# A gated delta-rule recurrence on one core: the third block of the older row turned first, and ScalarE's line in another order

## What is computed

```python
q, k, v = (silu(conv4(x @ W.T) + b) for W, b in ...)     # k also times 64 ** -0.5
a = sigmoid(x @ Wa.T + ba)                               # a decay for every value column
beta = sigmoid(x @ Wb.T + bb)
def step(S, ins):
    q_t, k_t, v_t, a_t, b_t = ins
    read = einsum('bhk,bhkv->bhv', k_t, S)
    err = read - v_t
    S = a_t[:, :, None, :] * S - b_t[:, :, None, None] * k_t[..., None] * err[:, :, None, :]
    return S, einsum('bhk,bhkv->bhv', q_t, S)
o = layernorm(o) * ln_w + ln_b
o = (o * sigmoid(x @ Wg.T)) @ Wo.T
```

## Time and profile before

| what | us |
|---|---|
| median of three runs | 1928.45 |
| the profiled execution, device time | 1928.56 |
| its span in the trace | 1926.7 |
| busy PE, PEld | 1698.9, 1438.6 |
| busy DVE, ACT, POOL | 1402.2, 1002.4, 703.8 |

### The profile page before, as it was taken

How to read it: one execution, slowest core, us unless ns; L and a number is a source line. 1 busy time by engine, 2 the same in 40 slices (tenths; PEclk the granted TensorE clock), 3 DMA queues, 4 the chain that set the end, 5 groups by cost and what they waited for, 6 DMA issues and landing times. The chain is left out here.

```text
span 1926.7 us, 42128 instructions
## 1 busy us (share of the span) xinstructions
PE 1698.9 (88%) x15318; PEld 1438.6 (75%) x15318; DVE 1402.2 (73%) x3422; ACT 1002.4 (52%) x2618; POOL 703.8 (37%) x1037
## 2 busy tenths in 40 slices
PE   4599999899999999999988598999999999988795
PEld 3477778787887878777776465788888888768794
DVE  4688777877788777887774475677777777754577
ACT  2355655555555655555543354566666666641353
POOL 5455345543555335543451121122222222223553
PEclk9799999999999999999988798999999999998798
DMA  6122331223222332323311793111111111123222
GB/s 215 54 55 64 75 86 49 69 62 81 66 55 65 74 86 53 69 64 75 86 48 21 164 123 1 24 34 35 35 34 35 34 34 35 34 45 108 58 85 76
DMA packets 168772, 123.69 MB, mean 64 GB/s; under 512 B 44372, under 2 KB 148888, under 8 KB 167672
## 3 DMA queue, kind: packets, MB, share of 16 engines
q1 hardware_dynamic: 166072, 115.87, 28.1%
q0 software_dynamic: 2496, 5.13, 0.8%
HBM read 102.83 MB, written 18.12 MB: 63 GB/s over the span
## 5 line engine op out<-in xcount | busy, mean ns | idle before, releaser
L590 POOL TENSOR_TENSOR kfull<-kt,pair_rows 128x512 f32<-128x512 f32 x128 | 143.4, 1121 | 517.6 <-ACT kt L378 513.9
L358 PE MATMUL ps<-xT,taps 128*128 128x128 f32 x2048 | 277.7, 279 | 0.1
L850 ACT COPY wt<-ps 32x128 f32<-32x128 f32 x512 | 131.2, 256 | 263.9 <-PE ps L745 257.7
L1658 POOL TENSOR_TENSOR b_yT<-b_yT,b_recipT 64x256 f32<-64x256 f32 x128 | 110.0, 859 | 431.0 <-ACT b_yT L1609 422.4
L358 PEld LDWEIGHTS ps<-xT,taps 128*128 128x128 f32 x2048 | 259.4, 197 | 7.6 <-issue 7.2
L893 DVE TENSOR_TENSOR prod<-ps,mt 128x128 f32<-128x128 f32 x512 | 147.4, 288 | 78.4 <-PE ps L756 62.8
L1676 DVE TENSOR_REDUCE b_nmax<-ps 128x1 f32<-128x128 f32 (+7 forms) x256 | 194.1, 758 | 8.8
L745 PE MATMUL ps<-ident,w 128*128 128x128 f32 x512 | 162.9, 318 | 35.0 <-ACT wt L850 18.5
L896 DVE TENSOR_REDUCE w<-prod 128x32 f32<-128x128 f32 x512 | 146.6, 286 | 17.5
L1603 ACT ACTIVATE b_prob_long<-ps,b_nmax 128x1024 f32<-128x1024 f32 (+3 forms) x128 | 122.1, 954 | 70.7 <-DVE b_nmax L1676 70.7
L745 PEld LDWEIGHTS ps<-ident,w 128*128 128x128 f32 x512 | 87.9, 172 | 85.1 <-DVE w L896 74.5
(11 more groups left out here) (302 smaller groups left out, 3834.6 us busy)
## 6 DMA issues: line engine op xcount, KB each, us to landing
decay<-ends_dram SPq DMA_DIRECT2D x256, 128.0 KB
b_recipT<-recips_dram SPq DMA_DIRECT2D x64, 256.0 KB, 3.8
gn<-near_dram SPq DMA_DIRECT2D x32, 384.0 KB, 6.8
slots_dram<-zero SPq DMA_DIRECT2D x1, 9216.0 KB, 65.4
rr<-rates_dram SPq DMA_DIRECT2D x32, 256.0 KB, 4.5
sq<-rstd_dram SPq DMA_DIRECT2D x16, 512.0 KB, 3.7
wtap<-in_taps SPq DMA_DIRECT2D x4, 1024.0 KB, 11.7
f_w<-in_f_w SPq DMA_DIRECT2D x2, 2048.0 KB, 10.6
```

Source lines behind the costliest of these rows:

```text
L358: mm = pe.matmul(part, lhsT=taps[:, tap, t * P:(t + 1) * P], rhs=xT[:, :, columns(at_next) - LOOK + tap:columns(at_next) - LOOK + tap + TS ...
L590: nc.gpsimd.tensor_tensor(kfull[:, n % 4, :, :], kt[:, n % 2, :].unsqueeze(1).to_broadcast([P, G, P]), cst["pair_rows"][:, :].unsqueeze(2) ...
L850: nc.scalar.copy(wt[rows, b, :], ps[rows, 2, 0:P]).then_inc(wt_kept[b], 1)
```

## The change

Four things, all in the order of work; nothing is computed otherwise, and one tiny evaluation per block is added.

1. **PE's line.** The older row's turn 2 comes first, then `start` of the younger row, then take-off 2, and slot 0 only behind it.
2. **The ring.** Item `a1` goes from slot 3 of j = 1 to slot 0 of j = 2, in front of `wo`, and `a3` from slot 3 of j = 2 to slot 0 of j = 3, in front of `g0`.
3. **ACT's line.** `put_back` goes from the end of a half chunk to right behind `keep` 2. The diagonal factors go from j = 3 and 4 to j = 5 and 7.
4. **The table of Silu.** At the end of j = 4 ACT evaluates Silu on one column into a new tile, `ready`.

```diff
+        ready = sb("ready", [P, NS])
...
-                ["q0.0"], ["q0.1"], ["b", "a0"], ["n", "a1", "p1"],
-                ["wo.0"], ["wo.1"], ["a2"], ["a3", "p2"],
-                ["g0.0"], ["g0.1"], ["c0"], ["p3"],
+                ["q0.0"], ["q0.1"], ["b", "a0"], ["n", "p1"],
+                ["a1", "wo.0"], ["wo.1"], ["a2"], ["p2"],
+                ["a3", "g0.0"], ["g0.1"], ["c0"], ["p3"],
...
+                    if cy >= 0:
+                        turn(cy, y, 2)
                     start(cc, x)
                     if cy >= 0:
-                        turn(cy, y, 2)
+                        take_off(cy, y, 2)
                     ring(0)
-                    if cy >= 0:
-                        take_off(cy, y, 2)
                     turn(cc, x, 0)
...
                         keep(cy, y, 2)
+                    if cc >= 1:
+                        put_back(cc - 1, x)
                     ring(0)
...
-                    if cc >= 1:
-                        put_back(cc - 1, x)
                     if j == 0:
                         act_norm(act, both, f)
-                    if j in (3, 4) and f < NS - 1:
-                        act_diagonal(act, f, 1 - f % 2, j - 3)
+                    if j == 4 and f < NS - 1:
+                        nc.scalar.activation(ready[:, f:f + 1], cst["eps"][:, 0:1], ACT.Silu)
+                    if j in (5, 7) and f < NS - 1:
+                        act_diagonal(act, f, 1 - f % 2, (j - 5) // 2)
```

## The result

| | before | after |
|---|---|---|
| median, us (4 runs each) | 1928.42 | 1982.32 |
| lowest and highest | 1924.8 to 1928.5 | 1978.1 to 1983.98 |
| first to last group of state products in the trace | 964.72 | 1018.08 |
| one block of the recurrence (median) | 61.16 | 64.66 |

The account below looks back on a forecast made before the run. PE was taken to have the least slack, with 80.5 us of waits on DVE and ACT. A loss of 2.85 us per block, 42.8 us in fifteen blocks, plus 4 in the last, on 1928.6 gave about 1975 us; range 1934 to 2002.

Parts of the forecast that it names:

- likeliest case: Whole kernel: a loss, with a time between 1955 and 1990 us; chance 0.6, giving the forecast of 1975 us.
- What bounds the kernel: Recurrence: PE has the least slack, waiting 80.5 us; no order of the same work can win more than 80 us.
- PE's line: Heads: the turn ahead of start costs +0.83 or +0.84 us at j = 0, 4, 5; little at j = 1, 2, 6, 7.
- four late heads: Heads of j = 0, 3, 4, 5, where DVE's reduce ends after PE is free: 0.84, 0.4, 0.4, 0.1 us per block.
- The term of j = 1: At j = 1 only start covers ACT's norm; take-off 2's wait becomes 0.8 us, adding 0.25 us.
- `a1`: The product of j = 1 stops waiting (0.8 us), but the later drain delays DVE in j = 2: gain 0.1 us.
- `a3`: At j = 3 PE stalls 0.77 us and take-off 0 is held back some 0.35 us; j = 3 adds 0.4.
- Table load: At the end of j = 4 the load costs nothing; j = 5 gains 0.65 us and loses 0.83 at its head.
- Diagonal factors: At j = 6 take-off 2 waits about 0.35 us for them; +0.55 us taken there and +0.4 in j = 7.
- The clock case: Head of j = 0: a 2.1 us stall lowers the clock every block, 1.5 us more each, 1999 us; chance 0.08 with worse.
- The faster case: Heads: new stalls replace ones that come anyway, what is freed stays free, 2.1 us per block, 1896 us; chance 0.13.

Follow-up runs that it names:

- e7: The changed kernel with DVE's solve 2 of the next older row put in front of update: 1941.43 us, 1.016 of the kernel before.
- e3: The kernel before with only a1 and a3 moved: 1896.48 us, 0.9921 of the kernel before.
- e14: The changed kernel with PE's line of before and the hold (POOL's key product at j = 0 waits until update is done): 1887.27 us, 0.9877 of before.
- e6: The kernel before with PE's new order at the heads of j = 1, 2, 6 and 7 only: 1949.6 us, 1.0112 of before.
- e8: The changed kernel with slot 0 back ahead of take-off 2, the turn still first: 1949.99 us, 1.0127 of the kernel before.
- e1: The changed kernel with PE's line of before (start, turn 2, slot 0, take-off 2): 1914.09 us, 1.0017 of the kernel before.
- e2: The kernel before with only PE's line changed (turn 2, start, take-off 2, slot 0): 1978.3 us, 1.0353 of the kernel before.
- e4: The kernel before with only the table load (Silu on one column) and the diagonal factors moved: 1924.01 us, 1.0063 of the kernel before.

## Why the prediction was right, point by point

The forecast was 1975 us, slower; measured are 1982.32 us, inside the range and inside the likeliest case. Its sum was 2.85 us per block (its terms add up to 2.84) against 3.50 measured, half chunk by half chunk, forecast first: j = 0 0.84 and 0.38, j = 1 0.25 and 0.42, j = 2 -0.1 and 0.21, j = 3 0.4 and 0.54, j = 4 0.4 and 0.50, j = 5 0.1 and 0.38, j = 6 0.55 and 0.38, j = 7 0.4 and 0.67.

- **What bounds the kernel: right, with a wrong ceiling.** The turn needs a `w` that DVE makes only behind `update`. The product's waits and L735's are gone, and e7 shows that the turn's hang on DVE's order. Their total, 96.0 us where "about 80" was said, is near in part by luck: the four late heads have 63 us of it, not 82 (j = 0 stalls 1.5 us, not 2.1), and 28 us are at the later turns of j = 2 and 7, which weren't forecast. And "no order of the same work can win more than these 80 us" doesn't follow: e3 and e14 win mostly what no bracket shows.
- **PE's line: right in sign, wrong in where.** The text put nearly all of it on the four late heads and said that "the heads cost nothing, or 0.1 to 0.4 us" at j = 1, 2, 6 and 7. This step failed: e6 has half of the loss there. What it missed is mostly that the take-off ahead of slot 0 waits for its `keep` with only `start` as cover (j = 1 and 2 are 0.94 and 0.52 us longer in e6); e8 prices that at 1.6%. The turn's place costs 2.5% (e8 over e14), or 1.1% over e1 with its collision. The term of j = 1 is the clearest: e8 takes 0.92 us off there, where the sum had 0.25 for the norm, although the wait of 0.8 us behind it was foretold (0.83). By the table the late heads were summed nearly right (1.74 us forecast, 1.80 measured) and the other four were not (1.10 and 1.68), which is nearly all of the sum's miss of 0.65. These columns hold the other parts of the change as well.
- **`a1`: near; `a3`: right only with the new PE order.** "A gain of 0.1 us out of the 0.8" stands against 0.29 us at j = 2 in e3, by the chain that the text walked. "`a3` costs twice" is wrong with PE's line of before, where j = 3 is 0.48 us shorter (e3). With the new line it fits: j = 3 takes 7.31 us in after and 6.86 in e2, whose `a3` stands where it stood, and the turn stalls 0.54 us where 0.77 was said. So the same move wins with one order of PE and costs with the other. In after DVE waits longer for the drain of `a1`, up to 1.5 us, as the text had it:

```profile
608.35 0.43 DVE L474 TENSOR_SCALAR di<-ex 128x512 f32<-128x512 f32 x1 [1.50 <-ACT ex L424]
...
609.48 0.33 PE L746 MATMUL ps<-ident,w 128*128 128x128 f32 x1 [0.30 <-DVE w L899]
...
610.72 0.33 PE L746 MATMUL ps<-ident,w 128*128 128x128 f32 x1 [0.47 <-DVE w L899]
```

  The two waits behind it, 0.30 and 0.47 us, eat most of what the product won. They are 0.36 and 0.47 us in e3, so the give-back belongs to the move of `a1` and comes with either order of PE.
- **Table load: right.** It costs nothing at the end of j = 4, and turn 1 of j = 5 waits no more. The first Silu stands right behind the load, so the extra 1380 ns that the Trainium skill gives (ScalarE: Activation LUTs, What ACT_TABLE_LOAD costs) is not to be seen in this trace:

```profile
627.91 1.28 ACT L878 ACT_TABLE_LOAD   x1
...
629.20 0.20 ACT L878 ACTIVATE ready<-eps 128x1 f32<-128x1 f32 x1
629.42 0.26 ACT L851 COPY wt<-ps 32x128 f32<-32x128 f32 x1
```

- **Diagonal factors: half right.** The wait of the take-off at j = 6 was put at 0.35 and is 0.38 us. The sum had 0.4 us in j = 7, put down to a late DVE, where e4 shows 0.52 by what looks like the second collision, and nothing for them at j = 0, where they cost 0.94 us in e4. In after the collision does not come about: POOL's product starts 0.63 us behind L518 (588.03 against 587.40 us), when L518 has just ended after its 0.61 us.
- **The clock case came in one block of fifteen** in after, not in each. The stall at the head of j = 0 is 1.3 to 1.6 us in one piece, less than the 2.1 us that the text had, and the granted clock behind it stays 1.00 (the last block not counted, as above); in the first of the fifteen the stall is 1.76 us, the clock falls to 0.50, and the half chunk takes 10.09 us in place of 8.28. Its turn and window, and a window of a usual block:

```profile
135.01 0.33 PE L746 MATMUL ps<-ident,w 128*128 128x128 f32 x1 [1.76 <-DVE w L899]
```

```profile
136.00:138.50 2.50, 2.50 (x21) 2.38 (x18) 1.79 (x6) 0.11 (x1) 0.00 (x0) 0.50 0.49 108
589.18:596.67 7.49, 7.49 (x73) 7.13 (x74) 4.58 (x13) 2.47 (x9) 0.00 (x0) 1.00 0.42 107
```

  In e2 the stall there is 1.83 us in nearly every block, and the clock falls behind it in 2 of 15. In e1 and e4 it falls more often, behind two waits of 0.65 and 1.44 us in a row.
- **The faster case** failed as its own text had it: at the late heads the reduce ends after PE is free. But its sum of what is freed was not far off: e14, which has PE's line of before and the hold, wins 1.2% where 1.7% was put.

## What to carry to other kernels

On an engine that runs its list in order, the item that depends on the fewest late things goes first: here `start` needs `update` alone and the turn needs a solve besides. Between a step and the one that needs its result by way of another engine, leave enough work as cover for the worst thing that can stand in that engine's line, not for the usual one. Bundled edits hide each other: three of the four parts win 1.2% when a small hold is added, and the fourth alone loses 3.5%, so try them apart. And the sum of the recorded waits is neither the ceiling of what an order can win nor the measure of what one has won: e14 takes 23.3 us off the recurrence and 5.3 us off the waits.

## What the runs showed of the hardware

- **DVE and POOL hold each other up on this pair.** Which of the two starts 0.04 us ahead decides whether DVE's L518 takes 0.61 or 1.47 us, and POOL's `kfull` 1.48 or 1.04. The Trainium skill (SBUF — State Buffer, SBUF: two separate sides) says that a vector operation with two inputs on SBUF and a GpSimd operation that reads SBUF share a pair of ports as an exclusive lock, kept for the whole instruction by whichever starts first; the trace agrees. It can show in a line whose minimum, median and maximum lie far apart, as L518's 621, 1472 and 1490 ns in e4.
- **The granted clock can fall behind the same head in some blocks and not in others**: in 5 of 15 in e4, 9 in e1, 2 in e2 and 1 in after, with the same instructions in each block, at some 1.5 to 1.8 us each. What decides between the blocks was not found.
- **One kernel, four medians**: before took 1928.42, 1912.01, 1926.35 and 1910.09 us beside the four groups of runs, 1% apart, with nearly all runs of a group within 0.3% of its median. For differences of a percent or less only ratios inside a group say anything.
